# Two half-used projections of an attention block as 64-row tiles in one step, and four residual tiles in the feed-forward part

## The chip, the cores and the metric

One Trainium2 chip, one of its cores. The metric is the device time of one execution in microseconds, as the median of several runs; lower is better.

## The reference

`x` is 16 sequences of 256 rows by 512. A gated cross-attention block and a gated feed-forward block follow each other:

```python
x = x + tanh(g_xattn[0]) * xattn(layernorm(x), ctx_1024, pos, pos, Wq, Wkv, Wout, bout)
x = x + tanh(g_ffn[0]) * ffn(layernorm(x), gate_w, up_w, down_w, expert_weight, ln_gamma, ln_beta)

# xattn: 32 heads of 16
q = x @ Wq ; k, v = split(ctx @ Wkv) ; q, k = axial_rope(q, pos), axial_rope(k, pos)
attn = softmax(q k^T / 4) v ; return attn @ Wout + bout
# ffn
h = square(relu(x @ up_w)) ; shared = h @ down_w
moe = (x @ expert_weight) * sum(top2(x @ gate_w))
y = shared + moe ; return (y - mean) * rsqrt(var + 1e-5) * ln_gamma + ln_beta
```

## The kernel before

Every product of two float32 matrices is made of three passes over rounded parts ("hi" and "lo"): hi by hi, lo by hi, hi by lo (`PASSES`). A projection of a 128-row tile is therefore 3 matmuls for each 128-row chunk of its contraction: 6 for K and V (context of 256, `CC` = 2 chunks) and 12 for Q and O (512, `KC` = 4 chunks). A name with `<` at its end is the first half (2 chunks, 6 matmuls) of such a Q or O.

The first part of the program is the attention. Blocks of one sequence each (two tiles of 128 rows) run through `iteration(i)`, 16 steps each (`STEPS`), one step for two heads. In each step TensorE makes

- "first logits" (`logits_a`, L1211, bank pair pA): 4 matmuls on 48 rows, two of them on rows 0 and up and two on rows 64 and up. VectorE reduces them to row maxima (`maxima`, L1534, tile mneg). They run `DELAY` = 3 steps ahead of what follows, and the next first logits wait for the maxima of these (`max_done`), since pA holds one step only;
- "second logits" (`logits_b`, L1227, bank pair pB): 4 matmuls on 50 rows, with the maxima in the stack of rows. ScalarE turns them into exponentials (L1012, tile probs);
- in the steps of `VALUES`, the product with v (`times_v`, L1239, bank pO), 16 matmuls;
- the jobs of that step in the table `SCHEDULE`, in its order. A job is a product (`product`, L1113), a transpose (`turn`, L1120) or one of two small ones (`b0`, `b1` at L1195 spread reciprocals over the rows; `m0`, `m1` at L1187 turn maxima). X is the transposed, normalised input, Q, K, V the projections, qT and kT the transposed and rotated q and k, O the output projection. `LAG` says which block a job of iteration i belongs to.

Three banks serve the jobs, P, M and T (`BANK`). A job waits until the one before it in its bank was taken away. ScalarE and VectorE take it in the step after the job, VectorE always behind the maxima of that step: 2 operations for K and Q (the rotation, L1456 and L1459), 1 for an X, kT, qT, O, b or m. V is taken by ScalarE alone. VectorE also has layer norm statistics (L1411, L1416) and their use (L1420, tile xn) in fixed steps, and 3 operations on the denominators (`reciprocals`, L1480 to L1484) in the steps of `RECIPROCALS`. GpSimd makes the inverse standard deviation between the two parts of a layer norm (L811, L813, tile rstd), adds the two halves of each rotation (`rope_sum`, L818), and makes the low part of the attention result (`rest_av`, L803). Its order is fixed: inverse deviation of the second tile, rotation sum of K0, `rest_av` of half 0, rotation sum of Q0, and so on. SyncE issues all transfers, about 0.65 us each, in one fixed order.

The second part is the feed-forward, 8 blocks of 512 rows in a loop. TensorE makes the hidden layer in banks pO and pP, the down projection in pA and pB and the expert product in pT. While block j runs, block j-1 is normalised: VectorE sums (L1609), takes statistics, scales with gamma (L1618) and makes the output with the residual (L1623, tile fres). GpSimd adds beta to that residual tile (L902). There are two residual tiles, so that the third is loaded when the first output is there. After the last block the same work stands alone at the end.

The order in which GpSimd does this, and the table that sets the steps:

```python
for u in range(UT):                 # L902 and L811, L813, once for each tile
    for_output(j - 1, u, done + u + 1)     # beta, then inverse deviation
```

Of the kernel before, what the change touches and what calls it, by code (L numbers as in the profile page):

```python
# [26 lines left out]
P = 128  # L27
# [10 lines left out]
KC = D // P  # L38
# [43 lines left out]
    14: ("V0",),  # L82
# [15 lines left out]
}  # L98
VALUES = {2: 0, 5: 1, 6: 2, 9: 3, 10: 4, 12: 5, 14: 6}
RECIPROCALS = {14: 0, 5: 1}  # L100
# [38 lines left out]
def first_maxima(b, u):  # L139

    return isinstance(b, int) and b == 0 and u < STEPS - DELAY

# [35 lines left out]
def flamingo_gated(nc, x, ctxT, posT, g_x, g_f, wq, wkv, wout, bout, gate, up, down, wexp, gamma, beta, out):  # L178
# [6 lines left out]
    with ExitStack() as stack:  # L185
# [155 lines left out]
        gt_raw = sb2("gt_raw", [P, KC, NEXP])  # L341
        second.close()
# [16 lines left out]
        f_lo = sem("f_lo")  # L359
        o_done = sem("o_done")  # L360
# [73 lines left out]
        fres_in = [sem(f"fres_in{k}") for k in range(2)]  # L434
# [93 lines left out]
        def _(sp):  # L528
# [138 lines left out]
            def first_tiles():  # L667
# [7 lines left out]
                sp.wait_ge(taken[BANK["V0"]], number("V0", B - 1))  # L675
# [58 lines left out]
            def fblock(j, first_block=False, last=False):  # L734
                if not first_block:

                    for u in range(UT):
                        n = (j - 1) * UT + u
                        if u >= 2:
                            sp.wait_ge(out_made, n - 1)  # L740
                            alone(sp)
                            sp.dma_start(out_d[n - 2], y_s[:, u - 2, :]).then_inc(out_out[u - 2], INC)
                        sp.dma_start(fres[u % 2][:], x1_d[n]).then_inc(fres_in[u % 2], INC)
                    for u in range(UT - 2, UT):
# [29 lines left out]
        def _(pool):  # L774
# [45 lines left out]
            def split_ctx(b, par):  # L820
                pool.wait_ge(ctx_in, INC * (b + 1))
                hi, lo = ctx_s[par]
                if some(b - 1):
                    pool.wait_ge(done[BANK["V0"]], number("V0", b - 2))
# [73 lines left out]
            def for_output(j, u, count):  # L898

                r = fres[u % 2]  # L900
                pool.wait_ge(fres_in[u % 2], INC * (2 * j + u // 2 + 1))
                nc.gpsimd.tensor_tensor(r[:], r[:], g_beta[:], ALU.add).then_inc(fres_made, 1)  # L902
                ffn_inv_std(count)
# [3 lines left out]
            def fblock(j, first_block=False, last=False):  # L907
                done = 2 * UT * j
                if not first_block:
                    for u in range(UT):  # L910
                        for_output(j - 1, u, done + u + 1)
# [9 lines left out]
            for u in range(UT):  # L921
                for_output(NB - 1, u, 2 * UT * NB - UT + u + 1)
# [178 lines left out]
        def _(pe):  # L1101
# [59 lines left out]

            def compute(name, b, par, psum, half=None):
# [4 lines left out]
                elif name[0] == "Q":  # L1167
                    last = product(psum, lambda a, c: xnT[a][:, c, :], lambda w, c: wq_s[w][:, c, :], KC, half)
                elif name[0] == "K":
                    pe.wait_ge(ctx_split, 2 * b + 2)  # L1170
                    last = product(psum, lambda a, c: ctx_s[par][a][:, c, t * P:(t + 1) * P],
                                   lambda w, c: wk_s[w][:, c, :], CC, half)
                elif name[0] == "V":
                    last = product(psum, lambda a, c: ctx_s[par][a][:, c, t * P:(t + 1) * P],
                                   lambda w, c: wv_s[w][:, c, :], CC, half)
                elif name[0] == "O":
                    pe.wait_ge(at_lo, 2 * b + (1 if half == 0 else 2))
                    cut = slice(t * P, (t + 1) * P)
                    last = product(psum, lambda a, c: rest(b, c // 2)[:, c % 2, cut] if a else aT_hi[:, c, cut], lambda w, c: wo_s[w][:, c, :], KC, half)
# [51 lines left out]
            def times_v(b, par, g):  # L1231
                pe.wait_ge(exp_done, STEPS * b + 2 * g + 2)
                if g == 0:
                    pe.wait_ge(taken[BANK["V0"]], number("V0", b))
# [20 lines left out]
            def iteration(i, par):  # L1255
                for s in range(STEPS):
                    if s >= DELAY and within(i + 1):
                        logits_a(i + 1, (par + 1) % 2, s - DELAY)
                    elif s < DELAY and within(i):
                        logits_a(i, par % 2, STEPS - DELAY + s)  # L1260
                    if within(i):
                        logits_b(i, par % 2, s)
                    if s in VALUES and within(i):
                        times_v(i, par % 2, VALUES[s])
                    elif s == 0 and within(i - 1):
                        times_v(i - 1, (par + 1) % 2, GROUPS - 1)
                    for name in names_at(i, s):
                        job(name, i, par)
# [101 lines left out]
        def _(dve):  # L1370
# [168 lines left out]
            def iteration(i, par):  # L1539
                for s in range(STEPS):  # L1540
# [70 lines left out]
            def norm_y(j, u, count):  # L1611
# [7 lines left out]
                                               ALU.mult).then_inc(z_made, 1)  # L1619
                dve.wait_ge(z_made, n + 1)  # L1620
                dve.wait_ge(rstd_made, NT + count)
                dve.wait_ge(fres_made, n + 1)
                nc.vector.scalar_tensor_tensor(y, y, rstd[:, 0:1], fres[u % 2][:], ALU.mult,  # L1623
# [101 lines left out]
```

## Time and profile before

| | us |
|---|---|
| median of 3 runs | 1567.92 |
| lowest and highest | 1567.05, 1567.99 |
| the profiled execution, its own time | 1566.75 |
| its span | 1564.9 |
| TensorE busy | 1515.9 (97%) |
| VectorE busy | 980.2 (63%) |
| ScalarE busy | 635.0 (41%) |
| GpSimd busy | 337.9 (22%) |

The span is that of the instructions; 1.9 us of the execution lie around it. In the slices of the span TensorE is at nine tenths or more almost throughout, and its clock too, but for the first slices and one near 700 us. The transfers are busiest up to 780 us (the attention) and low after it.

### The profile page before, as it was taken

To read this page: it belongs to the slowest core of one execution; us is meant where nothing else is said; L and a number is where in the kernel's file an instruction comes from. 1 tells how busy PE (TensorE), PEld (TensorE's weight loads), DVE (VectorE), ACT (ScalarE), POOL (GpSimd) and SP (SyncE) were. 2 spreads that over 40 slices of the span, in tenths; PEclk is the share of its full clock that TensorE was granted. 3 is DMA by queue.
4 is the path that set the end of the run, shared out by engine and by line. 5 is a ranking of instruction groups with operands and counts; after the bars stand their busy time and mean duration, and the time that the engine had idled before them with its cause. 6 is when DMAs were issued, how large, how long until landed. Compare 5 with 4: busy or idle time off the path is not lost.

```text
span 1564.9 us, 25920 instructions
## 1 busy us (share of the span) xinstructions
PE 1515.9 (97%) x9498; PEld 1125.0 (72%) x9498; DVE 980.2 (63%) x1416; ACT 635.0 (41%) x962; POOL 337.9 (22%) x406
## 2 busy tenths in 40 slices
PE   7789999999999999979999999999999999999997
PEld 6556666666666666646787888878888888788886
DVE  7788888888888888755655436435354264453524
ACT  4365665655555666665432222222222222222221
POOL 5323233333333333112101002001020020110202
PEclk9699999999999999999999999999999999999999
DMA  6645555555555555544411001101011010010101
GB/s 174 142 98 141 134 137 138 131 142 139 135 135 143 127 127 136 121 134 120 147 61 35 27 21 47 35 15 47 21 35 47 1 54 27 22 40 21 55 0 41
DMA packets 80623, 131.11 MB, mean 84 GB/s; under 512 B 21624, under 2 KB 35064, under 8 KB 80504
## 3 DMA queue, kind: packets, MB, share of 16 engines
q1 hardware_dynamic: 80504, 129.48, 32.4%
q8 instruction: 80, 1.31, 0.4%
q14 instruction: 39, 0.32, 0.1%
HBM read 51.17 MB, written 16.78 MB: 43 GB/s over the span
## 4 chain that ended last, share of the span: by engine, by line
PE 88%; DVE 7%; issue 2%; POOL 1%; ACT 1%; DMA 0%; SPq 0%; POOLq 0%; DVEq 0%; ACTq 0%
PE pP L1113 17%; PE pT L1113 11%; PE pA L1314 11%; PE pO L1113 11%; PE pB L1314 11%; PE pA L1211 7%; PE pO L1239 7%; PE pB L1227 3%; PE pM L1113 3%; DVE mneg L1534 3%; PE pP L1120 2%; PE pM L1120 2%; PE pT L1195 1%; PE pM L1281 1%; PE pM L1187 1%
## 5 line engine op out<-in xcount | busy, mean ns | idle before, releaser
L1534 DVE TENSOR_REDUCE mneg<-pA 128x4 f32<-128x1024 f32 x250 | 305.7, 1223 | 97.7 <-PE pA L1211 93.2
L1012 ACT ACTIVATE probs<-pB 128x1024 f32<-128x1024 f32 x249 | 255.8, 1027 | 213.2 <-PE pB L1227 203.3
L811 POOL TENSOR_SCALAR var_eps<-meanvar 128x1 f32<-128x1 f32 x96 | 34.6, 360 | 986.1 <-DVE meanvar L1416 985.9
L1637 DVE TENSOR_TENSOR relu<-relu 128x512 f32<-128x512 f32 x128 | 88.4, 690 | 252.3 <-ACT hid L1066 252.3
L1314 PE MATMUL pA<-dn,hid 128*128 128x512 f32 x768 | 197.1, 392 | 1.7 <-DVE hid L1639 1.5
L1314 PE MATMUL pB<-dn,hid 128*128 128x512 f32 x768 | 195.0, 389 | 0.0
L1113 PE MATMUL pP<-fT,up 128*128 128x512 f32 x768 | 188.5, 394 | 0.0
L1113 PE MATMUL pO<-fT,up 128*128 128x512 f32 x768 | 184.7, 389 | 0.0
L1314 PEld LDWEIGHTS pA<-dn,hid 128*128 128x128 f32 x768 | 142.9, 188 | 34.4 <-DVE hid L1639 5.1
L1113 PEld LDWEIGHTS pO<-fT,up 128*128 128x128 f32 x768 | 144.0, 188 | 30.3 <-issue 0.4
L1314 PEld LDWEIGHTS pB<-dn,hid 128*128 128x128 f32 x768 | 144.1, 188 | 30.0
L1113 PEld LDWEIGHTS pP<-fT,up 128*128 128x128 f32 x768 | 142.0, 188 | 30.2
L1211 PE MATMUL pA<-stk,stq 48*128 48x256 f32 x1000 | 129.2, 337 | 17.0 <-DVE mneg L1534 13.6
L1211 PEld LDWEIGHTS pA<-stk,stq 48*128 48x128 f32 x1000 | 76.7, 190 | 91.1 <-issue 58.8
L1239 PE MATMUL pO<-probs,v 128*17 128x256 f32 x2048 | 138.1, 388 | 0.0
L1059 ACT ACTIVATE relu<-pO 128x512 f32<-128x512 f32 x64 | 38.3, 598 | 241.3 <-PE pO L1113 241.3
L1059 ACT ACTIVATE relu<-pP 128x512 f32<-128x512 f32 x64 | 38.3, 598 | 193.3 <-PE pP L1113 193.3
L1227 PE MATMUL pB<-stq,stk 50*128 50x256 f32 x996 | 101.6, 283 | 1.9 <-DMA stq<-low 1.9
L1113 PE MATMUL pT<-wo,aT_hi 128*128 128x512 f32 x256 | 96.5, 418 | 1.2 <-DVE numer L1472 0.6
L1113 PE MATMUL pT<-ex,fT 128*128 128x512 f32 x384 | 92.3, 389 | 0.0
L1639 DVE TENSOR_TENSOR hid<-relu,hid 128x512 fp32r<-128x512 f32 x128 | 88.6, 693 | 4.4
L1113 PE MATMUL pP<-wq,xnT 128*128 128x512 f32 x336 | 90.9, 406 | 0.0
(200 smaller groups left out, 1989.8 us busy)
## 6 DMA issues: line engine op xcount, KB each, us to landing
stk<-kT SPq DMA_DIRECT2D x180, 128.0 KB, 2.9
stq<-qT SPq DMA_DIRECT2D x180, 128.0 KB, 2.9
fres<-x_scratch SPq DMA_DIRECT2D x34, 256.0 KB, 2.9
xin<-x SPq DMA_DIRECT2D x32, 256.0 KB, 2.9
numer<-av_s SPq DMA_DIRECT2D x128, 64.0 KB, 2.4
xres<-x SPq DMA_DIRECT2D x32, 256.0 KB, 2.9
x_scratch<-xres SPq DMA_DIRECT2D x32, 256.0 KB, 2.4
out<-y_s SPq DMA_DIRECT2D x32, 256.0 KB, 2.0
```

Of the source, the lines that this page charges most:

```text
L811: nc.gpsimd.tensor_scalar_add(var_eps[:], meanvar[:, 1:2], EPS).then_inc(ve_made, 1)
L1012: nc.scalar.activation(probs[:, s % 4, :, :, :].rearrange("p a b s -> p a (b s)"), psum[:, :, :], ACT.Exp).then_inc(exp_done, 1)
L1059: nc.scalar.activation(relu[m % 2][:], pU[m % 2], ACT.Relu).then_inc(relu_made, 1)
L1113: last = nc.tensor.matmul(dst, lhs(a, c), rhs(w, c), start=(c == 0 and (a, w) == PASSES[0]), stop=(c == chunks_ - 1 and (a, w) == PASSES[-1]))
L1120: last = nc.tensor.transpose(dst[:, c * P:(c + 1) * P], src(c), ident[:])
L1211: last = nc.tensor.matmul(psum[:, q, t * S:(t + 1) * S], st_q[par][rows, s, t * P:(t + 1) * P], st_k[par][rows, s, :], start=True, stop=True)
L1227: last = nc.tensor.matmul(psum[:, q, t * S:(t + 1) * S], st_k[par][rows, s, t * P:(t + 1) * P], st_q[par][rows, s, :], start=True, stop=True)
L1239: last = nc.tensor.matmul(pO[32 * j:32 * j + HD + 1, 0:S], v_s[par][:, t, 4 * g + j, :], probs[:, (2 * g + j // 2) % 4, j % 2, t, :], star ...
L1314: last = nc.tensor.matmul(acc[u], hid[m % 2][x_][:, u * P:(u + 1) * P], dn_s[w][:, m, :], start=(m == 0 and k == 0), stop=(m == MC - 1 and ...
L1534: nc.vector.tensor_reduce(mneg[par][:, :, 2 * u:2 * u + 2].rearrange("p t q -> p q t"), psum[:, :, :].rearrange("p q (t k) -> p q t k", t= ...
L1637: nc.vector.tensor_tensor(r[:], r[:], r[:], ALU.mult).then_inc(sq_made, 1)
L1639: nc.vector.tensor_tensor(hid[m % 2][1][:], r[:], hid[m % 2][0][:].bitcast(F32), ALU.subtract).then_inc(hid_lo, 1)
```

## The change

- Step 4 held V1 alone. It now holds V0 and the second half of Q0 as a pair (`PAIRS`, `paired`). Each of their 12 matmuls on 128 rows is cut into two on 64 rows: between first and second logits V0 uses rows 0 to 63 and Q0 rows 64 to 127, behind the second logits the two change sides. V0 goes to bank T, Q0 to bank P. The second dozen waits until the first is done (`rows_done`).
- V1 takes V0's place in step 14, in bank P.
- Q0's first half moves from step 2 to 3, X1 from 5 to 6, Q1's first half from 7 to 8, where b1 stands between the halves. In steps 10 and 12 two jobs change places.
- VectorE: the layer norm of the second tile moves from steps 2 and 3 to 3 and 4, the reciprocals from 14 and 5 to 12 and 4.
- Feed-forward: 4 residual tiles instead of 2. SyncE issues all four loads first and the four stores behind them. GpSimd's order in the loop is as it was; behind the last block it adds beta to all four tiles first.

```diff
 SCHEDULE = {
-    2: ("Q0<", "b0"),
-    3: ("m1", "Q0"),
-    4: ("V1",),
-    5: ("kT0", "X1"),
-    6: (),
-    7: ("K1", "Q1<"),
-    8: ("Q1", "b1"),
+    2: ("b0",),
+    3: ("Q0<", "m1"),
+    4: ("V0", "Q0"),
+    5: ("kT0",),
+    6: ("X1",),
+    7: ("K1",),
+    8: ("Q1<", "b1", "Q1"),
...
-    10: ("qT0", "O0<"),
+    10: ("O0<", "qT0"),
...
-    12: ("m0", "qT1"),
+    12: ("qT1", "m0"),
...
-    14: ("V0",),
+    14: ("V1",),
...
+PAIRS = (
+    (("V0", "Q0"), (4, "first logits"), (4, "second logits")),
+)
...
-RECIPROCALS = {14: 0, 5: 1}
+RECIPROCALS = {12: 0, 4: 1}
...
+            def paired(n, i, par, swapped):
+                if swapped:
+                    pe.wait_ge(rows_done, pair_number(n, i))
...
+                    rows = slice(HALF_ROWS, P) if (k == 1) != swapped else slice(0, HALF_ROWS)
...
+                for c in range(CC):
+                    for a, w in PASSES:
...
+                        for psum, rows, half, bank, lhs, rhs, _ in sides:
+                            at = c + (CC if half == 1 else 0)
+                            last = nc.tensor.matmul(psum[:, :], lhs(a, at)[rows, :], rhs(w, at)[rows, :],
+                                                    start=opens and half != 1, stop=closes and half != 0)
...
+                    pieces((s, "first logits"), i, par)
                     if within(i):
                         logits_b(i, par % 2, s)
+                    pieces((s, "second logits"), i, par)
...
-                    if s == 2 and within(i + 2) and not first:
+                    if s == 3 and within(i + 2) and not first:
                         ln_statistics(i + 2, 1)
-                    elif s == 3 and within(i + 2) and not first:
+                    elif s == 4 and within(i + 2) and not first:
                         ln_apply(i + 2, 1)
...
             fblock(NB - 1, last=True)
             for u in range(UT):
-                for_output(NB - 1, u, 2 * UT * NB - UT + u + 1)
+                add_beta(NB - 1, u)
+            for u in range(UT):
+                ffn_inv_std(2 * UT * NB - UT + u + 1)
```

VectorE in one iteration, steps 3 to 5. Before (numer is the job b0 taken away, low is m1, rot_q and rot are Q0, den the reciprocals; each TENSOR_REDUCE opens a step):

```order
L1534 TENSOR_REDUCE mneg<-pA 128x2x2
L1472 TENSOR_TENSOR numer<-pT,numer 128x512
L1420 TENSOR_SCALAR xn<-xin,meanvar,rstd 128x512
L1534 TENSOR_REDUCE mneg<-pA 128x2x2
L1462 TENSOR_TENSOR low<-pM,low 16x256
L1456 TENSOR_TENSOR rot_q<-pP,cos_t 128x512
L1459 TENSOR_TENSOR rot<-pP,sin_t 128x512
L1534 TENSOR_REDUCE mneg<-pA 128x2x2
L1480 RECIPROCAL den<-den 64x64
L1482 CAST den_hi<-den 64x64
L1484 TENSOR_TENSOR den_lo<-den,den_hi 64x64
```

With the change:

```order
L1598 TENSOR_REDUCE mneg<-pA 128x2x2
L1536 TENSOR_TENSOR numer<-pT,numer 128x512
L1475 BN_STATS stats<-xin 128x6
L1480 BN_AGGR meanvar<-stats 128x2
L1598 TENSOR_REDUCE mneg<-pA 128x2x2
L1526 TENSOR_TENSOR low<-pM,low 16x256
L1484 TENSOR_SCALAR xn<-xin,meanvar,rstd 128x512
L1544 RECIPROCAL den<-den 64x64
L1546 CAST den_hi<-den 64x64
L1548 TENSOR_TENSOR den_lo<-den,den_hi 64x64
L1598 TENSOR_REDUCE mneg<-pA 128x2x2
L1520 TENSOR_TENSOR rot_q<-pP,cos_t 128x512
```

The statistics now stand in step 3 behind b0 instead of in step 2, xn and the reciprocals share step 4, and the rotation of Q0 stands in step 5.

TensorE, step 4. Before, from its first logits (pA) to those of step 5 (wv is V1's weight):

```order
L1211 MATMUL pA<-stk,stq 128x256 x4
L1227 MATMUL pB<-stq,stk 128x256 x4
L1113 MATMUL pT<-wv,ctx 128x512 x6
L1211 MATMUL pA<-stk,stq 128x256 x4
```

With the change, its beginning (of 24 matmuls on 64 rows the first six stand here; six more like them come before the second logits, twelve behind them):

```order
L1270 MATMUL pA<-stk0,stq0 128x256 x4
L1218 MATMUL pT<-wv0,ctx00 128x512
L1218 MATMUL pP<-wq0,xnT0 128x512
L1218 MATMUL pT<-wv0,ctx01 128x512
L1218 MATMUL pP<-wq0,xnT1 128x512
L1218 MATMUL pT<-wv1,ctx00 128x512
L1218 MATMUL pP<-wq1,xnT0 128x512
```

V0 (pT) and Q0 (pP) alternate, and no matmul on 128 rows is left in the step.

GpSimd behind the last feed-forward block. Before:

```order
L902 TENSOR_TENSOR fres<-fres,g_beta 128x512
L811 TENSOR_SCALAR var_eps<-meanvar 128x1
L813 TENSOR_TENSOR rstd<-var_eps,neg_half 128x1
L902 TENSOR_TENSOR fres<-fres,g_beta 128x512
L811 TENSOR_SCALAR var_eps<-meanvar 128x1
```

With the change:

```order
L917 TENSOR_TENSOR fres<-fres,g_beta 128x512 x4
L826 TENSOR_SCALAR var_eps<-meanvar 128x1
L828 TENSOR_TENSOR rstd<-var_eps,neg_half 128x1
L826 TENSOR_SCALAR var_eps<-meanvar 128x1
L828 TENSOR_TENSOR rstd<-var_eps,neg_half 128x1
```

The four additions of beta stand ahead of all four inverse deviations instead of one ahead of each.

## Rows read from the trace of the kernel before

**Rows 1.** Three stretches of one iteration: length, busy time of each engine, clock

```profile
613.02:625.85 12.83, 12.73 (x119) 8.18 (x118) 11.67 (x19) 8.17 (x12) 4.57 (x5) 1.00 0.53 120
625.85:632.16 6.31, 6.31 (x38) 4.59 (x38) 4.43 (x6) 2.45 (x4) 2.54 (x2) 1.00 0.69 167
640.37:645.05 4.68, 4.68 (x45) 3.05 (x45) 3.72 (x6) 3.27 (x5) 0.00 (x0) 1.00 0.91 214
```

**Rows 2.** Timeline of TensorE, steps 2 to 5: start, us, instructions

```profile
614.69 1.66 PE L1113 MATMUL pP<-wq,xnT 128*128 128x512 f32 x6
616.28 0.50 PE L1195 MATMUL pT<-low 32*128 32x256 f32 x2
616.71 0.51 PE L1211 MATMUL pA<-stk,stq 48*128 48x256 f32 x4
...
619.08 0.50 PE L1211 MATMUL pA<-stk,stq 48*128 48x256 f32 x4
...
619.76 1.65 PE L1113 MATMUL pT<-wv,ctx 128*128 128x512 f32 x6
621.34 0.50 PE L1211 MATMUL pA<-stk,stq 48*128 48x256 f32 x4
```

**Rows 3.** The same, the second logits of step 4 as two pairs

```profile
619.43 0.28 PE L1227 MATMUL pB<-stq,stk 50*128 50x256 f32 x2
619.55 0.28 PE L1227 MATMUL pB<-stq,stk 50*128 50x256 f32 x2
```

**Rows 4.** Timeline of VectorE, steps 2 to 6

```profile
615.91 0.69 DVE L1411 BATCH_NORM_STATS2 stats<-xin 128x6 f32<-128x512 f32 x1
616.79 0.18 DVE L1416 BATCH_NORM_AGGREGATE meanvar<-stats 128x2 f32<-128x6 f32 x1 [0.19 <-DVE stats L1411]
...
619.00 0.61 DVE L1420 TENSOR_SCALAR xn<-xin,meanvar,rstd 128x512 f32<-128x512 f32 x1
619.63 1.23 DVE L1534 TENSOR_REDUCE mneg<-pA 128x4 f32<-128x1024 f32 x1
620.77 0.40 DVE L1462 TENSOR_TENSOR low<-pM,low 16x256 fp32r<-16x256 f32 x1
621.10 0.67 DVE L1456 TENSOR_TENSOR rot_q<-pP,cos_t 128x512 f32<-128x512 f32 x1
...
623.43 0.53 DVE L1480 RECIPROCAL den<-den 64x64 f32<-64x64 f32 x1
...
624.57 1.23 DVE L1534 TENSOR_REDUCE mneg<-pA 128x4 f32<-128x1024 f32 x1
```

**Rows 5.** Timelines of GpSimd and VectorE: operations that meet

```profile
607.48 1.28 POOL L828 TENSOR_TENSOR ctx<-ctx_raw,ctx 128x512 fp32r<-128x512 f32 x1
607.93 1.12 DVE L1420 TENSOR_SCALAR xn<-xin,meanvar,rstd 128x512 f32<-128x512 f32 x1
...
618.03 1.29 POOL L818 TENSOR_TENSOR rot_k<-rot_k,rot 128x512 f32<-128x512 f32 x1
621.48 1.29 POOL L803 TENSOR_TENSOR rest<-numer,aT_hi 128x512 fp32r<-128x512 f32 x1 [2.16 <-ACT aT_hi L983]
...
697.32 1.40 POOL L803 TENSOR_TENSOR rest<-numer,aT_hi 128x512 fp32r<-128x512 f32 x1 [0.31 <-ACT aT_hi L983]
698.40 0.36 DVE L1482 CAST den_hi<-den 64x64 fp32r<-64x64 f32 x1
```

**Rows 6.** Timeline of the end of the program

```profile
1546.36 1.29 POOL L902 TENSOR_TENSOR fres<-fres,g_beta 128x512 f32<-128x512 f32 x1
1546.48 1.72 DVE L1623 SCALAR_TENSOR_TENSOR y_s<-y_s,rstd,fres 128x512 f32<-128x512 f32 x1 [0.82 <-POOL rstd L813]
...
1553.79 1.52 PE L1314 MATMUL pB<-dn,hid 128*128 128x512 f32 x6
...
1558.21 0.68 DVE L1609 TENSOR_TENSOR y_s<-pB,y_s 128x512 f32<-128x512 f32 x1
...
1561.59 0.75 DVE L1623 SCALAR_TENSOR_TENSOR y_s<-y_s,rstd,fres 128x512 f32<-128x512 f32 x1 [0.82 <-POOL rstd L813]
```

More of the change, by code:

```diff
@@ L141, in first_maxima, with pair_at, pair_number @@
     return isinstance(b, int) and b == 0 and u < STEPS - DELAY
+def pair_at(n, i):
+    names = PAIRS[n][0]
+    return names if within(i) and all(live(x.rstrip("<"), i) for x in names) else ()
+def pair_number(n, i):
+    order = sorted(range(len(PAIRS)), key=lambda k: PAIRS[k][1])
+    return (sum(bool(pair_at(k, j)) for j in range(i) for k in order)
+            + sum(bool(pair_at(k, i)) for k in order[:order.index(n) + 1]))
 def before(names, i):
@@ L341, in flamingo_gated @@
         gt_raw = sb2("gt_raw", [P, KC, NEXP])
+        fres += [sb2(f"fres{k}", [P, D]) for k in range(2, UT)]
         second.close()
@@ L359, in flamingo_gated @@
         f_lo = sem("f_lo")
+        rows_done = sem("rows_done")
         o_done = sem("o_done")
@@ L433, in flamingo_gated @@
         z_made = sem("z_made")
-        fres_in = [sem(f"fres_in{k}") for k in range(2)]
+        fres_in = [sem(f"fres_in{k}") for k in range(UT)]
         fres_made = sem("fres_made")
@@ L737, in fblock @@
                     for u in range(UT):
[L738 to L744, printed above, removed]
+                        sp.dma_start(fres[u][:], x1_d[(j - 1) * UT + u]).then_inc(fres_in[u], INC)
+                    for u in range(UT):
                         n = (j - 1) * UT + u
@@ L823, in split_ctx @@
                 if some(b - 1):
-                    pool.wait_ge(done[BANK["V0"]], number("V0", b - 2))
+                    for name in ("V0", "V1"):
+                        pool.wait_ge(done[BANK[name]], number(name, b - 2))
                 alone(pool)
@@ L910, in fblock @@
                     for u in range(UT):
-                        for_output(j - 1, u, done + u + 1)
+                        add_beta(j - 1, u)
+                        ffn_inv_std(done + u + 1)
                 if not last:
@@ L921, in _ @@
             for u in range(UT):
-                for_output(NB - 1, u, 2 * UT * NB - UT + u + 1)
+                add_beta(NB - 1, u)
+            for u in range(UT):
+                ffn_inv_std(2 * UT * NB - UT + u + 1)
         @block.scalar
@@ L1162, in compute, with pieces @@
+            def pieces(place, i, par):
+                for n, (_, upper, lower) in enumerate(PAIRS):
+                    for swapped, at in enumerate((upper, lower)):
+                        if at == place and pair_at(n, i):
+                            paired(n, i, par, bool(swapped))
             def compute(name, b, par, psum, half=None):
@@ L1166, in compute @@
                     last = turn(psum, lambda c: xn[:, c * P:(c + 1) * P])
[L1167 to L1179, printed above, removed]
+                elif name[0] in "QKVO":
+                    inputs_of(name, b, half)
+                    last = product(psum, *factors(name, b, par), half)
                 elif name[0] in "qk":
@@ L1266, in iteration @@
                         times_v(i - 1, (par + 1) % 2, GROUPS - 1)
+                    together = {x for n in range(len(PAIRS)) for x in pair_at(n, i)}
                     for name in names_at(i, s):
-                        job(name, i, par)
+                        if name not in together:
+                            job(name, i, par)
                     if planned(tile_at, i, s) is not None:
@@ L1619, in norm_y @@
                                                ALU.mult).then_inc(z_made, 1)
+            def norm_y(j, u, count):
+                n = UT * j + u
+                y = y_s[:, u, :]
+                centre_y(j, u, count)
                 dve.wait_ge(z_made, n + 1)
```

47 lines of the change are left out of this document (38 added, 9 removed), and 4 rows, old and new, of the table BANK.

## The prediction, made before the changed kernel was run

> **What bounds the kernel now.** I read the busy shares first, then the slices, then the timeline of one iteration of the attention engine by engine. TensorE is busy for 97% of the span and VectorE for 63%, so a saving has to be one of TensorE's time, and it counts only while nothing else takes over. The timeline shows how close VectorE is. From the first logits of step 2 to those of step 7 an iteration takes 12.83 us, and TensorE is busy for 12.73 of them, but VectorE for 11.67 [rows 1]. At the end of this stretch VectorE is already the later one: its maxima of step 6 run from 624.57 to 625.80, and step 7 begins at 625.85 [rows 1, 4]. From step 7 to step 9 it takes 6.31 us and VectorE has 4.43 of work: there TensorE alone decides [rows 1]. Each step is a handshake: maxima begin 0.55 us after the first logits (619.08, 619.63), take 1.23, and the next first logits follow 0.05 after their end [rows 2, 4]. What VectorE does for the jobs stands between two maxima. So the question for each moved job is not only what TensorE needs for it, but whether VectorE still gets through its step.
>
> **TensorE's own sum, steps 2 to 6.** A product of 6 matmuls costs 1.59 us from its start to what follows (614.69 to 616.28) and 1.58 (619.76 to 621.34) [rows 2]. Six matmuls in FFN take 1.52 with the last one's 0.39 of latency in it, so one more costs 0.23, six 1.36 [rows 6]. The other 0.2 is the change between 128 rows and the narrower tiles. In the logits two matmuls on different rows run together: four take two slots of 0.12 (619.43, 619.55) [rows 3], and the first pair of a step that follows a product on 128 rows takes 0.1 longer (0.34 from first to second logits, 619.08 to 619.43 [rows 2, 3]). No row has such a pair with 512 columns. Its slot lies between 0.23, the price of one 512-column matmul, and 0.46, two of them with nothing shared. I take 0.23, since the nearest row, the 256-column pair, is fully shared.
>
> Removed: Q0's first half in step 2, 1.59; V1 in step 4 with both changes of rows, 1.58 + 0.2. Added: 12 slots of 0.23, 2.76, and about 0.1 for the wait on rows_done, which keeps the next weights from being fetched early (bounds 0 and 0.3; nothing shows such a wait of TensorE on itself). X1 only moves from step 5 to 6. TensorE would need 12.83 - 1.59 - 1.78 + 2.86 = 12.32 us, 0.5 less. This is what the pair is worth if TensorE stays the bound.
>
> **VectorE's sum, the same steps.** It does the same work as before in this stretch, but step 2 has lost the 1.59 us that used to hide some of it, and the statistics, xn and the reciprocals now come one after another. Prices from start to start: maxima 1.14 (619.63 to 620.77), m1's low part 0.33, a rotation operation 0.67 busy less the 0.07 by which neighbours overlap, 0.60; b0 the same; statistics 0.88 to the aggregate and 0.20 on; xn 0.62; reciprocals 1.14 (623.43 to 624.57) [rows 4]. From the first logits of step 2: 0.55, maxima and K0 2.34, then 1.14 + 0.60 + 1.08 = 2.82 for step 3, 1.14 + 0.33 + 0.62 + 1.14 = 3.23 for step 4, 2.34 for step 5 with Q0, and 1.23 + 0.05 for the last maxima. That is 12.56. VectorE would be the bound by 0.24, and the stretch still 0.27 shorter than before.
>
> Two of these operations now meet GpSimd.
> - xn. GpSimd goes from the inverse deviation straight to K0's rotation sum, which ended at 619.32, 3.41 us after the statistics began (615.91) [rows 4, 5]. xn at 619.00 just missed it. Where an xn did meet a GpSimd operation it ended 0.29 after that (608.76 and 609.05) and took 1.12 [rows 5]. Now the statistics begin at 4.63 of the stretch, the sum ends at 8.04, and xn would start at 7.18: it ends at 8.33 instead of 7.80, 0.53 late.
> - The reciprocals then start at 8.33. GpSimd's rest_av began 2.05 after the second logits of step 4 (619.43 and 621.48) [rows 3, 5]. These come later now, behind the first six slots: 2.08 + 2.37 + 0.34 + 6 x 0.23 = 6.17. So rest_av runs from 8.22 to 9.51, and the cast den_hi, due at 8.90, falls into it. The one row of such a meeting has the cast end 0.04 after GpSimd (698.72 and 698.76) [rows 5]. That moves what follows by up to 0.39; I take 0.3, as it is one row.
>
> The stretch becomes 12.56 + 0.53 + 0.3 = 13.39, 0.56 longer than before. The pair's saving lies under it: TensorE is ready for step 6 about 1 us before VectorE, so a slot of up to 0.31 would cost nothing either.
>
> By the Trainium skill ("SBUF — State Buffer", on the shared port pair between the engines) the one of VectorE and GpSimd that comes second waits until the first is finished and only then does its whole work. By that xn would end its full 0.55 after GpSimd, 0.26 later than the row says, which would be an estimate of 3.4 us more over 13 iterations. The row decides, and the sum goes by 0.29.
>
> **The other steps.** Step 7 keeps K1 alone: 0.34 + 0.34 + 1.58 = 2.26. Step 8 has Q1's first half, b1, then Q1's second: 0.68 + 1.59 + 0.43 (616.28 to 616.71 [rows 2]) + 1.58 = 4.28. Together 6.54 against 6.31 [rows 1]: 0.23 more, because b1 splits the product and the rows change twice more. Steps 12 and 13 take 4.68 [rows 1]; VectorE now needs 0.55 + 1.14 + 0.67 (O0) + 1.14 (reciprocals) + 1.23 + 0.05 = 4.78, 0.10 more. Steps 10, 14, 15, 0 and 1 keep their content. SyncE's queue: m0's low part comes about 1.1 us later in step 13, behind the reciprocals and qT1, and all transfers behind it in that queue too: the maxima for the next iteration's second logits, stq, and the reciprocals for b0. I count nothing, for they had 1.5 us and more in hand; if b0, which is itself asked for 1.6 us earlier, found them late, each iteration would lose up to 0.5 us.
>
> **Iterations.** Pairs are made in iterations 0 to 13. In 1 to 13 all of this holds: 13 x (0.56 + 0.23 + 0.10) = 11.6. Iteration 0 has neither b0 nor reciprocals, so VectorE is free and TensorE's 0.5 is saved.
>
> **The feed-forward part.** TensorE stays near full there, and VectorE's work lies beside it, so in the loop two more tiles give nothing. At the end VectorE stands alone. Its output operation takes 1.72 us while GpSimd adds beta (1546.36 to 1547.65), three times in a row, and 0.75 when it does not (1561.59) [rows 6]. Now all additions are done before. One tile costs VectorE 1561.59 + 0.75 - 1558.21 = 4.13, and TensorE delivers one about every 4.1, so VectorE keeps up. The last sum starts soon after TensorE's last matmul at 1555.31 instead of at 1558.21: 2.8 saved, at most 2.9.
>
> **Sum:** 11.6 - 0.5 - 2.8 = +8.3 us. The profiled execution took 1566.75, so 1575.1; the median of the runs is 1.2 above it, and for a median I say 1576.2.
>
> **Rivals.**
> - *The engines do not meet as I say, and the pair pays (faster).* The place is steps 3 to 6. If xn and the cast run as they did in iterations where they missed GpSimd, the stretch is 12.56, 0.27 less. With 0.23 and 0.10 more elsewhere the iterations come out even: 13 x 0.06 - 0.5 - 2.8 = -2.5, so 1565.4; with the first half of Q1 costing no more than before it is -5.5, 1562.4. For it: VectorE is busy for only 63% and the xn of rows 4 lost nothing. Against it: the arithmetic puts xn 0.9 us inside a GpSimd operation. It decides once VectorE's added waits in the stretch stay under 0.3 us. Chance 0.26.
> - *Only xn waits.* 13 x 0.59 - 3.3 = +4.4, 1572.3. This is part of my own forecast's range.
> - *The pair does not do what it says.* If two tiles of 512 columns shared nothing, 24 slots would take 5.5 us instead of 2.76, TensorE would be the later one again by about 1.7 us, and 14 iterations would cost 24 more: near 1600. Against it: the logits' pairs are shared. Chance 0.05.
> - *A transfer becomes the wait* (b0, above): up to 13 x 0.5 = 6.5 on top, 1582.7. Chance 0.08.
>
> **Chances.** My forecast, VectorE bound with one or both waits, 0.61; the rivals as given. A measurement of this kernel tells about 0.2%, 3.1 us, from no change. The faster case lies around that limit, so it gives 0.18 to faster and 0.08 to same; some 0.05 of my own case, if the waits are small, is same too. Slower: 0.69. The 8 in 10 range runs from 1563.5 (half of the faster case) to 1583 (the late transfer).
>
> **What would show it.** Right: in the changed profile the stretch from step 2 to 7 takes 13.1 to 13.5 us, TensorE waits for mneg at steps 6 and 7, xn takes about 1.1 us in both places, den_hi in step 4 about 0.5; steps 7 and 8 together 6.5; the output operations at the end 0.75. The two halves of the pair start together every 0.23 us. Wrong: no wait of TensorE on mneg in these steps and an iteration below 42.05 us; or slots well over 0.3 us in the pair; or a wait on a transfer ahead of b0 or the second logits.

## The result, and the profile after

The changed kernel takes 1576.71 us (median of 4 runs, 1575.67 to 1578.0), the kernel before 1567.49 in the same comparison (4 runs, 1565.71 to 1567.99). The ratio is 1.0062, with an interval of 1.0048 to 1.0076: slower by 9.2 us. The forecast was 1576.2.

| | us |
|---|---|
| the profiled execution, its own time | 1577.67 |
| its span | 1575.9 |
| TensorE busy | 1519.5 (96%) |
| VectorE busy | 988.9 (63%) |
| GpSimd busy | 338.9 (22%) |

TensorE is busy 3.6 us longer than before and the span is 11.0 longer: most of the new time is waiting of TensorE. The first table to make is one of steps. These are the distances between the starts of the first logits in one iteration from the middle of the program, worked out from the traces, of the two kernels and of five of the experiments below:

| step | before | after | no_pair | inv_late | q1_whole | both | both_no_pair |
|---|---|---|---|---|---|---|---|
| 2 | 3.68 | 2.09 | 2.09 | 2.09 | 2.09 | 2.09 | 2.09 |
| 3 | 2.38 | 2.47 | 2.47 | 2.47 | 2.47 | 2.47 | 2.47 |
| 4 | 2.26 | 3.44 | 3.65 | 3.44 | 3.44 | 3.44 | 3.65 |
| 5 | 2.68 | 3.10 | 2.71 | 2.16 | 3.10 | 2.16 | 2.24 |
| 6 | 1.83 | 2.33 | 2.33 | 2.25 | 2.33 | 2.25 | 2.25 |
| 7 | 3.61 | 2.26 | 2.25 | 2.25 | 2.25 | 2.25 | 2.27 |
| 8 | 2.70 | 4.29 | 4.29 | 4.29 | 4.04 | 4.04 | 4.08 |
| 12 | 2.41 | 2.46 | 2.46 | 2.46 | 2.46 | 2.46 | 2.46 |
| 13 | 2.27 | 2.26 | 2.26 | 2.26 | 2.26 | 2.26 | 2.26 |
| iteration | 42.07 | 42.90 | 42.71 | 41.87 | 42.65 | 41.63 | 41.98 |

The changed kernel's stretches from step 2 to 7 and from step 7 to 9, to be held against the first two of [rows 1] (length, then busy time of TensorE, its weight loads, VectorE, ScalarE and GpSimd, the clock, the transfers), and one whole iteration:

```profile
623.99:637.41 13.42, 12.54 (x131) 8.46 (x131) 12.73 (x19) 8.14 (x12) 4.44 (x5) 1.00 0.59 144
637.41:643.96 6.55, 6.55 (x38) 4.51 (x38) 4.78 (x6) 2.64 (x3) 3.90 (x4) 1.00 0.54 121
600.00:642.90 42.90, 42.02 (x373) 27.84 (x372) 36.67 (x48) 25.26 (x36) 13.56 (x15) 1.00 0.56 133
```

The first stretch is 13.42 us instead of 12.83. TensorE was busy for 12.73 of the 12.83, and now stands for 0.88 of the 13.42. VectorE has the same 19 operations, but is busy for 12.73 instead of 11.67. The 1.06 us more are not work. The timeline of VectorE in steps 4 and 5 shows where they lie, as in [rows 4]:

```profile
630.66 0.40 DVE L1526 TENSOR_TENSOR low<-pM,low 16x256 fp32r<-16x256 f32 x1
630.99 1.29 DVE L1484 TENSOR_SCALAR xn<-xin,meanvar,rstd 128x512 f32<-128x512 f32 x1
632.20 0.54 DVE L1544 RECIPROCAL den<-den 64x64 f32<-64x64 f32 x1
632.77 0.87 DVE L1546 CAST den_hi<-den 64x64 fp32r<-64x64 f32 x1
633.68 0.22 DVE L1548 TENSOR_TENSOR den_lo<-den,den_hi 64x64 fp32r<-64x64 f32 x1
633.82 1.21 DVE L1598 TENSOR_REDUCE mneg<-pA 128x4 f32<-128x1024 f32 x1
```

And GpSimd in the same stretch, to be held against [rows 5]:

```profile
630.16 0.57 POOL L828 TENSOR_TENSOR rstd<-var_eps,neg_half 128x1 f32<-128x1 f32 x1
630.70 1.30 POOL L833 TENSOR_TENSOR rot_k<-rot_k,rot 128x512 f32<-128x512 f32 x1
632.32 1.27 POOL L818 TENSOR_TENSOR rest<-numer,aT_hi 128x512 fp32r<-128x512 f32 x1 [0.32 <-ACT aT_hi L1000]
```

K0's rotation sum runs from 630.70 to 632.00. xn was issued at 630.99 and ends at 632.28, 0.28 behind it. `rest_av` runs from 632.32 to 633.59, and the cast den_hi, issued at 632.77, ends at 633.64. There are no idle gaps on VectorE here: the waits are inside the two operations, which makes them look like work (1.29 and 0.87). The engine that really stands is TensorE:

```profile
628.55 0.51 PE L1270 MATMUL pA<-stk,stq 48*128 48x256 f32 x4
628.89 0.39 PE L1218 MATMUL pT<-wv,ctx 64*128 64x512 f32 x1
628.89 0.40 PE L1218 MATMUL pP<-wq,xnT 64*128 64x512 f32 x1
629.12 0.39 PE L1218 MATMUL pT<-wv,ctx 64*128 64x512 f32 x1
629.13 0.39 PE L1218 MATMUL pP<-wq,xnT 64*128 64x512 f32 x1
...
631.98 0.41 PE L1270 MATMUL pA<-stk,stq 48*128 48x256 f32 x4
...
635.09 0.50 PE L1270 MATMUL pA<-stk,stq 48*128 48x256 f32 x4 [0.87 <-DVE mneg L1598]
```

At step 6 it waits 0.87 us for VectorE's maxima. The two 64-row halves of the pair start together (628.89), and the next two 0.23 later.

### The profile page after: what moved, and what is told of

It is laid out like the page before. It is cut to its first block, busy times and chain, and to the rows that moved or that the text cites. A ratio compares the mean times of both kernels' runs of the same rounds, so it can differ in the third digit from the quotient of the medians.

```text
span 1575.9 us, 26279 instructions
## 1 busy us (share of the span) xinstructions
PE 1519.5 (96%) x9666; PEld 1132.3 (72%) x9666; DVE 988.9 (63%) x1416; ACT 637.0 (40%) x962; POOL 338.9 (22%) x406
## 4 chain that ended last, share of the span: by engine, by line
PE 80%; DVE 12%; SPq 3%; issue 2%; ACT 1%; DMA 1%; POOL 1%; DVEq 0%; POOLq 0%; ACTq 0%
PE pP L1130 15%; PE pA L1378 11%; PE pB L1378 11%; PE pO L1130 11%; PE pT L1130 10%; PE pO L1299 5%; PE pA L1270 5%; DVE mneg L1598 5%; PE pM L1130 3%; PE pB L1286 3%; PE pP L1137 2%; SPq L572 1%; PE pM L1137 1%; DVE xn L1484 1%; DVE den_hi L1546 1%
## 5 line engine op out<-in xcount | busy, mean ns | idle before, releaser
L1083 ACT ACTIVATE hid<-relu 128x512 fp32r<-128x512 f32 x128 | 80.9, 632 | 11.2
```

Source lines behind the costliest of these rows:

```text
L1083: nc.scalar.activation(hid[m % 2][0][:], relu[m % 2][:], ACT.Square).then_inc(hid_hi, 1)
```

## The experiments

The theory: in steps 4 to 6 VectorE is the bound, made so by two meetings with GpSimd; the split of Q1 in step 8 costs a further 0.2 us per iteration; the pair's saving lies hidden under both; the feed-forward's end gives back nearly 3 us. The main rivals: VectorE's own work there is the bound, meetings or not; or the pair itself costs the time. Each kernel was compared with the kernel before in its own batch: 1566.59 us (15 runs) for the first four, 1566.84 (18) for the next three, 1566.76 (15) for the last two.

### The two parts of the change alone: ffn_only and attn_only

ffn_only is the kernel before with the changed feed-forward part; attn_only is the changed kernel with the old one.

```diff
-fres_in = [sem(f"fres_in{k}") for k in range(2)]
+fres_in = [sem(f"fres_in{k}") for k in range(UT)]
...
             for u in range(UT):
-                for_output(NB - 1, u, 2 * UT * NB - UT + u + 1)
+                add_beta(NB - 1, u)
+            for u in range(UT):
+                ffn_inv_std(2 * UT * NB - UT + u + 1)
```

> The kernel before with the four residual tiles alone. Theory (the gain lies in the tail, where GpSimd's addition of beta held three output operations of VectorE): 2.8 us less than before, near 1564.7; the last four output operations take 0.75 us each and the last sum follows TensorE's last matmul within 0.2 us. Rival (the tail was bound by TensorE and the transfers, and the whole change's loss is even): no difference, 1567.5.

> The changed kernel with two residual tiles as before, so the attention part of the change alone. Theory: 2.8 us more than the changed kernel, 1579.5, about 12 more than before, all of it ahead of the feed-forward part; iterations 1 to 13 take 42.9 us instead of 42.07. Rival (the four tiles cost time in the loop, by their early loads): less than 1576.7.

ffn_only took 1565.34 us, a ratio of 0.9989 (0.998 to 0.9998); attn_only 1578.72, 1.0067 (1.0052 to 1.0083). The whole loss comes from the attention. In the profiled executions the way from the start of TensorE's last matmul of the down projection to the end of the span is 10.0 us in the kernel before and 7.15 in ffn_only and in the changed kernel, and the last output operations take 0.75 us each, as expected. The medians give less: 1.3 us for ffn_only and 2.0 between attn_only and the changed kernel. The interval of ffn_only reaches from 0.3 to 3.1 us, so it holds the 2.85 of the profile, but near its end.

### Four tiles, but beta and inverse deviation in turn at the end: beta_each

```diff
             for u in range(UT):
                 add_beta(NB - 1, u)
-            for u in range(UT):
                 ffn_inv_std(2 * UT * NB - UT + u + 1)
```

> The changed kernel with GpSimd's old order behind the last block (beta, then the inverse deviation, tile by tile); the four tiles and the early loads stay. Theory: the order alone makes the saving, so it is lost: 1579.5, output operations of 1.72 us. Rival (the early loads make it): 1576.7.

It took 1580.62 us, 1.0086 (1.007 to 1.0101), 3.9 above the changed kernel. Its last tiles, first GpSimd's and VectorE's operations that meet, then the last sum and the last output:

```profile
1570.75 1.26 POOL L917 TENSOR_TENSOR fres<-fres,g_beta 128x512 f32<-128x512 f32 x1
```

```profile
1570.88 1.69 DVE L1692 SCALAR_TENSOR_TENSOR y_s<-y_s,rstd,fres 128x512 f32<-128x512 f32 x1 [0.82 <-POOL rstd L828]
1572.48 0.68 DVE L1672 TENSOR_TENSOR y_s<-pB,y_s 128x512 f32<-128x512 f32 x1
...
1575.87 0.75 DVE L1692 SCALAR_TENSOR_TENSOR y_s<-y_s,rstd,fres 128x512 f32<-128x512 f32 x1 [0.82 <-POOL rstd L828]
```

The changed kernel at the same place, as in [rows 6]:

```profile
1568.48 0.75 DVE L1693 SCALAR_TENSOR_TENSOR y_s<-y_s,rstd,fres 128x512 f32<-128x512 f32 x1 [0.82 <-POOL rstd L828]
1569.16 0.69 DVE L1673 TENSOR_TENSOR y_s<-pB,y_s 128x512 f32<-128x512 f32 x1
...
1572.56 0.75 DVE L1693 SCALAR_TENSOR_TENSOR y_s<-y_s,rstd,fres 128x512 f32<-128x512 f32 x1 [0.82 <-POOL rstd L828]
```

With four tiles and the old order the output takes 1.69 again, and the last sum begins 3.24 us after the start of TensorE's last matmul (1569.24 to 1572.48), instead of 0.43 (1568.73 to 1569.16). So the four tiles give nothing by themselves. What they do is make room for the order in which GpSimd is done with beta before VectorE needs the tiles; with two tiles that order can't be had.

### The pair undone: no_pair

```diff
-PAIRS = (
-    (("V0", "Q0"), (4, "first logits"), (4, "second logits")),
-)
+PAIRS = ()
```

> The changed kernel without the pair: in the same steps V0 and the second half of Q0 are ordinary products on 128 rows. Theory: VectorE bounds steps 3 to 6, TensorE is ready 0.9 us early, and the 0.28 us by which step 4 and the start of step 5 get longer are covered: 1576.7, within 1.5 us; step 5 shorter by what step 4 is longer. Rival 1 (the 64-row tiles themselves cost time): faster than 1574. Rival 2 (the pair's saving reaches the end): 14 x 0.28 = 3.9 more, 1580.6.

It took 1576.07 us, 1.0059 (1.0043 to 1.0074): no difference from the changed kernel that the runs can tell. (In the profiles an iteration is 0.19 shorter without the pair, 42.71 and 42.90, and iterations 1 to 13 together 2.3; the medians show 0.6.) The rival that the pair itself costs the 9 us falls, and so does the hope that it brings something where it stands. The table of steps shows the trade. Step 4 is 0.21 longer on TensorE (3.65), but step 5 is 0.39 shorter (2.71), because one wait of VectorE is shorter. VectorE, then GpSimd:

```profile
500.36 1.28 DVE L1482 TENSOR_SCALAR xn<-xin,meanvar,rstd 128x512 f32<-128x512 f32 x1
501.56 0.53 DVE L1542 RECIPROCAL den<-den 64x64 f32<-64x64 f32 x1
502.13 0.70 DVE L1544 CAST den_hi<-den 64x64 fp32r<-64x64 f32 x1
```

```profile
500.06 1.29 POOL L831 TENSOR_TENSOR rot_k<-rot_k,rot 128x512 f32<-128x512 f32 x1
501.31 1.47 POOL L816 TENSOR_TENSOR rest<-numer,aT_hi 128x512 fp32r<-128x512 f32 x1
```

Without the pair's first dozen in front of them the second logits come earlier in the step, `rest_av` follows the rotation sum at once instead of 0.32 later, and the cast waits for 0.17 less. So in the changed kernel the pair makes the second meeting longer, while its saving lies under VectorE's waits. `rest_av` itself shows 1.47 instead of 1.27: it was issued at 501.31, while xn was still running until 501.64, and 1.14 of it lie after that. The waiting goes both ways.

### GpSimd's order mended: inv_late and clear_pool

inv_late puts K0's rotation sum ahead of the inverse deviation, since its inputs are ready first. clear_pool also puts Q0's sum ahead of `rest_av`.

```diff
                 if prepares:
-                    inv_std(b2 * TT + 2)
                     rope_sum(b2, "K0")
+                    inv_std(b2 * TT + 2)
...
-                if within(bt):
-                    rest_av(bt, 0)
                 if prepares:
                     rope_sum(b2, "Q0")
+                if within(bt):
+                    rest_av(bt, 0)
```

(The second hunk is in clear_pool alone.)

> The changed kernel with one exchange on GpSimd: K0's rotation sum before the inverse deviation of the second tile. xn then meets no GpSimd operation and takes 0.55 to 0.61 us instead of 1.29. Theory: the stretch from step 2 to 7 loses 0.7 us if the reciprocals' operations get through before rest_av begins (the cast is due just ahead of it, den_lo at the same moment), 1567.6; if den_lo is caught by rest_av, VectorE is held to its end as before and nothing is gained, 1576.5. Rival (TensorE or a transfer bounds the stretch): nothing, whatever den_lo does.

> The changed kernel with GpSimd's order K0's rotation sum, inverse deviation, Q0's rotation sum, rest_av of half 0. Neither xn nor the reciprocals meet a GpSimd operation. Theory: the stretch from step 2 to 7 takes 12.4 us instead of 13.43 and is bound by TensorE, 13 x 1.0 = 13 less: 1563.7, faster than before. Rival (VectorE's own work or a transfer bounds it): 12.9 or more, above 1570.

inv_late took 1563.41 us, 0.998 (0.9971 to 0.9989); clear_pool 1563.13, 0.9974 (0.9963 to 0.9984). Two exchanged calls on an engine that is busy for 22% of the time are worth 13.3 us and turn the loss of the change into a gain. The theory for inv_late had its price too low (1567.6): it counted the wait of xn alone, 0.7 us, and an iteration is 1.03 shorter. VectorE in inv_late, steps 4 and 5:

```profile
534.25 0.53 DVE L1484 TENSOR_SCALAR xn<-xin,meanvar,rstd 128x512 f32<-128x512 f32 x1
534.70 0.53 DVE L1544 RECIPROCAL den<-den 64x64 f32<-64x64 f32 x1
535.27 0.19 DVE L1546 CAST den_hi<-den 64x64 fp32r<-64x64 f32 x1
535.49 0.22 DVE L1548 TENSOR_TENSOR den_lo<-den,den_hi 64x64 fp32r<-64x64 f32 x1
535.70 1.23 DVE L1598 TENSOR_REDUCE mneg<-pA 128x4 f32<-128x1024 f32 x1
```

And GpSimd there:

```profile
530.29 1.29 POOL L833 TENSOR_TENSOR rot_k<-rot_k,rot 128x512 f32<-128x512 f32 x1 [7.27 <-DVE rot L1523]
...
533.42 0.57 POOL L828 TENSOR_TENSOR rstd<-var_eps,neg_half 128x1 f32<-128x1 f32 x1
535.58 1.27 POOL L818 TENSOR_TENSOR rest<-numer,aT_hi 128x512 fp32r<-128x512 f32 x1 [1.59 <-ACT aT_hi L1000]
```

The rotation sum runs 2.7 us before xn, and xn takes 0.53 instead of 1.29. The second meeting disappears with the first: the reciprocal now starts 0.88 us before `rest_av` (0.12 in the changed kernel), and the cast has ended (535.46) when that begins (535.58). It takes 0.19 instead of 0.87. den_lo is issued at 535.49, 0.09 ahead of `rest_av`, and takes its usual 0.22. So the second exchange, which clear_pool has on top, finds nothing left, and the two kernels agree in the iteration (41.87 and 41.85) and in the median. No run has the second exchange alone, so what each meeting costs by itself is read from the lengths of the operations and not from a run. The maxima run beside `rest_av` here at their usual length.

Which is the bound is also settled. One iteration of inv_late:

```profile
527.79:569.66 41.87, 41.87 (x376) 27.83 (x372) 35.32 (x48) 25.16 (x36) 13.64 (x14) 1.00 0.57 138
```

TensorE is busy for all of it. The rival that VectorE's own work bounds steps 2 to 6 falls: without the meetings they take 12.41 us, and VectorE's chain from the first logits of step 2 (527.25) to the end of the maxima of step 6 (539.25) takes 12.00, with the 0.05 of the handshake 12.05.

### Q1 in one piece again: q1_whole

```diff
-    8: ("Q1<", "b1", "Q1"),
+    8: ("Q1", "b1"),
```

> The changed kernel with step 8 as Q1 whole, then b1, instead of Q1's first half, b1, second half. Theory: step 8 takes 4.05 instead of 4.29 us, since two changes of rows go: 14 x 0.23 = 3.2 less, 1573.5. Rival (what follows in steps 9 to 11 waits for b1, which comes 1.4 us later): nothing, 1576.7.

It took 1573.96 us, 1.0044 (1.0029 to 1.0059), 2.75 below the changed kernel. Step 8 goes from 4.29 to 4.04 in some iterations and 4.08 in others, the iteration from 42.90 to 42.65 or 42.69; iterations 1 to 13 together are 2.9 shorter. b1 between the halves of Q1 is a cost that nothing hides, since TensorE alone is the bound there, in `637.41:643.96` above busy for all of 6.55.

### Both mended, with and without the pair: both and both_no_pair

> The changed kernel with GpSimd's order mended (K0's rotation sum ahead of the inverse deviation, Q0's ahead of the scaling of av) and Q1 whole again in step 8. Theory: the two meetings cost steps 4 to 6 about 1.05 us per iteration, the split of Q1 costs step 8 about 0.2, and the two lie in different stretches, so they add up: iteration about 41.65 us, some 3 us below the kernel with the mended order alone, near 1560.5 us. Rival: what step 8 saves comes back as a wait on the maxima in step 9 or on a transfer later; then no difference to the mended order alone, 1563.

> The kernel both without the pair: V0 and Q0's second half run one after the other in step 4, each on 128 rows. In the changed kernel itself the pair was worth nothing, since VectorE was the later engine in steps 4 to 6. Theory: with VectorE's two waits gone TensorE is the later one again in step 4, and the pair's slots (12 of 0.23 for two products of 1.6 less what the changes of rows cost) are felt: steps 4 to 6 about 0.3 to 0.5 us longer than in both, 14 iterations, 4 to 7 us, near 1566. Rival: VectorE is still the later one there; then within 1.5 us of both.

both took 1559.68 us, 0.996 (0.9947 to 0.9974): 7.1 us below the kernel before and 17 below the changed one. It is the fastest kernel of this document. both_no_pair took 1565.51, 0.9997 (0.9988 to 1.0006). The intervals don't overlap: here the pair is worth 5.8 us by the medians and 0.35 per iteration by the profiles (41.63 and 41.98), 4.9 in 14. The same edit brought nothing in the changed kernel. One iteration of both:

```profile
600.00:641.63 41.63, 41.63 (x373) 27.92 (x373) 35.42 (x49) 25.17 (x37) 13.57 (x14) 1.00 0.52 119
```

Where the pair's gain comes from shows in both_no_pair, where the two products stand one behind the other:

```profile
617.80 0.41 PE L1284 MATMUL pB<-stq,stk 50*128 50x256 f32 x4
618.14 1.66 PE L1128 MATMUL pT<-wv,ctx 128*128 128x512 f32 x6
619.63 1.54 PE L1128 MATMUL pP<-wq,xnT 128*128 128x512 f32 x6
621.11 0.50 PE L1268 MATMUL pA<-stk,stq 48*128 48x256 f32 x4
```

And in both, the pair's first matmul, the second logits in its middle, its first matmul behind them, and the logits of step 5:

```profile
613.17 0.39 PE L1218 MATMUL pT<-wv,ctx 64*128 64x512 f32 x1
...
614.55 0.41 PE L1286 MATMUL pB<-stq,stk 50*128 50x256 f32 x4
614.79 0.49 PE L1218 MATMUL pP<-wq,xnT 64*128 64x512 f32 x1
...
616.27 0.41 PE L1270 MATMUL pA<-stk,stq 48*128 48x256 f32 x4
616.51 0.42 PE L1286 MATMUL pB<-stq,stk 50*128 50x256 f32 x4
```

From 618.14 to 621.11 are 2.97 us for 12 matmuls on 128 rows. The 12 slots of the pair in both take 1.38 (613.17 to 614.55) and 1.48 (614.79 to 616.27), together 2.86. The streaming is the same, 12 times 0.23: two matmuls on 64 rows side by side take the slot of one on 128, and there are twice as many. What the pair saves is 0.11 here, 0.10 at the second logits of step 4 (0.24 from them to what follows instead of 0.34, 614.55 to 614.79 and 617.80 to 618.14) and 0.10 at the first logits of step 5 (616.27 to 616.51 instead of 621.11 to 621.45): in each case a change between 128 rows and narrower tiles that is no longer there. It is a saving of changes, not of matmuls. In the profiles steps 4 and 5 are 0.29 shorter with the pair; the other 0.06 of the 0.35 lie in steps 7 and 8 and are not explained.

## Why the prediction was right, and where it was not

The sum was made against the profiled execution: +8.3 us. Between the two profiled executions it is +10.9, between the medians +9.2. The changed kernel's profiled execution lies 1.0 above its median, that of before 0.7 below.

| term | predicted | measured |
|---|---|---|
| steps 2 to 6, per iteration | 13.39 (+0.56) | 13.42 (+0.59) |
| steps 7 and 8 | +0.23 | +0.24 |
| steps 12 and 13 | +0.10 | +0.04 |
| steps 9 and 10 | 0 | -0.04 |
| iterations 1 to 13 | +11.6 | +10.7 |
| iteration 0 | -0.5 | +0.4 |
| iteration 14 | 0 | +1.3 |
| the end | -2.8 | -2.9 |
| ahead of iteration 0 | 0 | +0.7 |
| iteration 15 and the feed-forward loop | 0 | +0.7 |

The last two rows are no effect of the change that the runs can tell: over the eleven profiles the first of these stretches varies by 1.5 us and the second by 1.8, in kernels that don't differ there too.

The forecast for the median, 1576.2, lies 0.5 us from the measured 1576.7. That is closer than its parts are: 0.9 too much in the middle iterations stands against 0.9 too little in iteration 0 and against 2.7 that the sum had at nothing, and the step from the profile to the median was forecast as +1.2 and is -1.0. The way, the cause and the size of the largest term were right; the last microseconds are luck.

**The meetings.** Of the xn step: the rotation sum was to end 8.04 us after the first logits of step 2, and ended at 8.01; xn was to end at 8.33, and ended at 8.29. `rest_av` was to run from 8.22 to 9.51, and ran from 8.33 to 9.60. The step of the prediction that placed each operation inside the other's time held, and inv_late shows that it is the cause.

Two sizes behind it were off, by half a microsecond each and in opposite directions. VectorE's own work without waits was put at 12.56 us; in inv_late the same chain takes 12.05. Three prices were too long and make 0.45 of the difference. xn was counted with 0.62 from start to start and takes 0.45: the row at 619.00 did not just miss the rotation sum, as the prediction says, but was held by it for its last part (it ended 0.29 us after it and took 0.61 instead of 0.53). The reciprocals were counted with 1.14 and take 1.00: in the row the maxima behind them stood for TensorE's logits (624.02, and 0.55 to 624.57). Step 3 was put at 2.82 and takes 2.68. The waits on the other side were put at 0.53 and 0.3, and cost VectorE 0.76 (xn, 1.29 instead of 0.53) and 0.62 (the reciprocals up to the maxima, 1.62 instead of 1.00). So 13.42 is 12.05 and 1.37, not 12.56 and 0.83, and that 13.39 came so near is luck: had both been too short, 13 iterations would have missed by 13 us.

For the cast I took 0.3, and it lost 0.68. The rows gave up to 0.39, and I went below that because I had one row only, which is no reason to go down; some 0.2 more are the places (issued at 8.78, not 8.90, with `rest_av` to 9.60, not 9.51). Of the 1.37 the stretch gets 1.02 back when the meetings go (13.43 to 12.41), for then TensorE is the bound.

**How long the one that comes second waits.** xn ended 0.28 us after GpSimd's operation, as the row of before had it (0.29), and 0.53 is its own work when nothing meets it. By the Trainium skill ("SBUF — State Buffer", section "SBUF: two separate sides", on the shared port pair) the one that starts first has the pair for its whole instruction and the other is blocked; read so, xn should have done its whole work after GpSimd had finished. The trace does not agree with that to the letter: about half of xn lies behind GpSimd's recorded end, of the cast 0.05 of 0.19, and of the output operation at the end of the program, in the kernel before, 0.55 of 0.75 (1547.65 to 1548.20). That the one that comes second, where it is held, is held for most of what is left of the other, and that each can be that one, the traces do show; whether the two ever proceed together can't be told from recorded ends. The prediction's estimate of what the rule would add, 0.26 in each of 13 iterations, is too high in any case: a later xn would be covered by the cast, which waits for `rest_av` either way. Only the cast's own 0.14 (0.19 instead of 0.05 behind it) would come on top, 1.8 us by the same kind of estimate.

**The pair.** Its slot was taken as 0.23, and is 0.23; the wait on rows_done was taken as 0.1, and the first slot behind it takes 0.33 (whether by the wait or by the change of sides, no run tells). TensorE's own sum was 12.32; inv_late and both have 12.41. That the pair's saving would lie under VectorE held: no_pair is no slower. In both_no_pair it shows.

**Step 8** cost what the sum said, for the reason that it gave (q1_whole). Of the 0.10 in steps 12 and 13 only 0.04 came, and steps 9 and 10, not in the sum, gave as much back.

**The signs.** The stretch lies within 13.1 to 13.5, steps 7 and 8 take 6.55, the output operations 0.75, and the pair's halves start together. TensorE stands for the maxima at step 6 but not at step 7, xn takes 1.29 and 1.17 instead of 1.1, and the cast 0.87 instead of 0.5.

**Iteration 0: the step that failed.** The prediction said that VectorE is free there and that TensorE's 0.5 is saved. The iteration is 0.4 longer instead (41.20 and 41.63). The part for which the 0.5 was forecast, from step 2 to 7, took 12.93 us before and takes 13.89 now, and TensorE stands for 1.50 of them; without that it would be 12.39, 0.5 less than before, though part of this is the clock, granted at 0.95 there before and at 1.00 now. (Elsewhere in the iteration 0.5 come back: step 9 had waited for GpSimd before, and no longer does.) ScalarE, then TensorE, in the changed kernel:

```profile
71.70 1.02 ACT L1029 ACTIVATE probs<-pB 128x1024 f32<-128x1024 f32 x1 [2.99 <-DMA stq<-av_s]
72.78 0.50 PE L1286 MATMUL pB<-stq,stk 50*128 50x256 f32 x4 [1.50 <-ACT probs L1029]
```

And before:

```profile
70.56 1.66 PE L1113 MATMUL pP<-wq,xnT 128*128 128x512 f32 x6
71.05 1.03 ACT L1012 ACTIVATE probs<-pB 128x1024 f32<-128x1024 f32 x1 [2.99 <-DMA stq<-av_s]
```

In iteration 0 alone, ScalarE's exponentials of steps 1 and 2 wait until the stack of the next sequence is loaded (a wait that stands in both kernels). Those of step 2 start at 71.05 before and at 71.70 with the change; the 0.65 between the two is the later begin of the attention in this execution (first logits at 44.37 and 45.03). The second logits of step 3 need them. Before, Q0's first half filled TensorE's time until then (70.56 to 72.15); now it stands for 1.50 us, and the saving is gone. no_pair (1.60), inv_late (1.70) and both (1.87) show the same wait. I read waits on transfers in an iteration from the middle only, and not in the first.

**Iteration 14** was left out of the sum. It is 1.3 us longer in the changed kernel's profile, but the profiles of kernels that don't differ there have 35.9 (inv_late) to 41.3 us (attn_only) for it. What varies is one wait and the clock behind it. The job b1 waits there: den_lo's transfer is issued at 679.42, lands about 2.1 us later, and b1 starts at 681.58. Then the clock decides. The changed kernel:

```profile
681.58 0.76 PE L1254 MATMUL pT<-low 32*128 32x256 f32 x2 [2.09 <-issue]
682.27 0.80 PE L1270 MATMUL pA<-stk,stq 48*128 48x256 f32 x4
```

```profile
677.00:687.00 10.00, 6.83 (x62) 4.17 (x66) 5.17 (x5) 4.79 (x7) 3.02 (x3) 0.66 0.56 136
```

inv_late:

```profile
666.48 0.47 PE L1254 MATMUL pT<-low 32*128 32x256 f32 x2 [1.01 <-issue]
666.88 0.50 PE L1270 MATMUL pA<-stk,stq 48*128 48x256 f32 x4
```

```profile
662.00:672.00 10.00, 7.70 (x90) 4.47 (x82) 6.34 (x6) 6.49 (x9) 3.79 (x3) 1.00 0.60 146
```

In the first the granted clock is 0.66 over these 10 us, so partly at the lower of its two levels (1.2 GHz), and the four logits take 0.80 us instead of 0.50; in the second it is 1.00. The kernel before had the fall too (a wait of 1.96 us at the same place, 0.66 from 665 to 675). What starts it was not tried. It is one reason why a single profiled execution of this kernel can't tell 2 us: inv_late's lies 3.7 below its own median.

**The rivals.** That the engines do not meet was the main one on the other side, at 1562.4 to 1565.4. inv_late and clear_pool are this case made real: 1563.4 and 1563.1. Its condition was not met in the changed kernel. Its time came near, but not for the reason that it gave: it had VectorE's 12.56 as the bound of steps 2 to 6, and without the meetings TensorE's 12.41 is the bound. That only xn waits did not come: in this kernel, where the one meeting goes, the other goes too. That b0 waits for a transfer in each iteration did not come: in the iteration from the middle TensorE stands for 0.88 us, 0.87 of them at step 6. A transfer is behind a wait that costs something new only in iteration 0.

## What to carry to other kernels

Before a saving on the busiest engine is counted, lay out the next engine's operations in their new order, with the third engine's beside them: where one of VectorE's operations on SBUF meets one of GpSimd's, the later can lose most of what is left of the earlier (here 0.76 of 1.01 us, and 0.68 of 0.82). The loss shows as a longer operation and not as idle time. Here one exchange in the order of the less busy engine removed it. Two matmuls side by side on 64 rows took the slot of one on all rows, so halving full contractions gained nothing in streaming; the gain was in the changes between tilings that went away, three tenths of a microsecond an iteration. An edit that was worth nothing while another engine was the bound was worth 5.8 us once that bound was gone, so judge the parts again after the mend. And when two terms of a sum are read from rows, take an operation's price from a row in which it neither waited nor was held.

## What was unexpected in the hardware

- Not every operation of VectorE is held by GpSimd. In no_pair the reciprocal ran at 501.56 beside `rest_av` in its usual 0.53 us, and in inv_late the maxima, which read PSUM, ran beside it in 1.23, while the cast of the same 64x64 numbers lost 0.68 in the changed kernel.
- The holding goes both ways: GpSimd's `rest_av`, issued 0.33 us before an xn ended, showed 1.47 instead of 1.27 us.
- xn, when it was held, ended 0.28 us after GpSimd's operation, though it takes 0.53 alone; the output operation of the feed-forward part ended 0.55 after it and takes 0.75 alone.
- 24 matmuls of 64 rows by 512 columns ran in 12 slots of 0.23 us, both halves of a slot within 0.01 us of each other.
